# Entry of layer two in a fused two-layer network: values, keys and masks of the first two units ahead of the gathered rows

## The chip, the cores and the metric

The kernel runs on one core of a Trainium2 chip. The metric is the device time of one execution in microseconds (us), the median over a few runs. The core has a matrix engine (TensorE, PE in the profile; its weight loads are PEld), a vector engine (VectorE, DVE), an activation engine (ScalarE, ACT), a general engine (GpSimd, POOL) and a queue engine (SyncE, SP), which here only issues DMA transfers. Each engine works through its own list of instructions in order, and they wait for one another by semaphores.

## The reference, cut to what matters

Two layers act on `x`, 128 sequences of 64 tokens of 128 numbers. Each layer is attention over a context followed by a mixture of experts. In the first layer the mixture sends each token to one of 8 experts; in the second it is a soft mixture of 16 projections with an attention of its own.

```python
x = x + tanh(g_xattn[0]) * L0_xattn(layernorm(x), ctx, ctx, ...)
x = x + tanh(g_ffn[0])   * L0_ffn(layernorm(x), ...)      # one of 8 experts for each token
x = x + tanh(g_xattn[1]) * L1_xattn(layernorm(x), ctx, ctx, mask, ...)
x = x + tanh(g_ffn[1])   * L1_ffn(layernorm(x), ...)      # 16 projections, weighed
```

`L1_xattn` is attention with 16 heads of width 8. Queries come from the normed `x`, keys and values from `ctx`, which does not depend on `x`. A causal mask and a padding mask are set on the scores before the softmax:

```python
q = query @ Wq.T + bq;  k = key @ Wk.T + bk;  v = value @ Wv.T + bv
scores = einsum('bhtd,bhsd->bhts', q, k) * 8 ** -0.5
scores = where(causal_mask | key_padding_mask, neg_inf, scores)
out = einsum('bhts,bhsd->bhtd', softmax(scores), v) @ Wo.T + bo
```

## The kernel before, in words

The 8192 tokens are 32 units of 256 tokens (4 sequences). Layer one's attention loops over the units. Its mixture scatters the token rows to DRAM sorted by expert, and a loop over 71 slots of 128 rows (`slots`) reads them in that order, computes, and stores them in `sorted_out`. Layer two takes the rows of a unit back with two indirect transfers (`gather`), which POOL issues once the last slots are stored. `upper_units` then runs layer two's steady loop (`body1`), in which the mixture of unit u is interleaved with the attention of the units u+1 to u+5. Each engine has such a body, written by hand.

Between the slots and `body1` stands the entry of layer two, an order written out by hand for every engine. It brings units 0 and 1 through attention and starts units 2 and 3. This entry alone is what the change touches. Its steps by name:

- `gather(v)` (POOL): the rows of unit v into `xin`. `first_stats` (DVE), `norm` (POOL) and `apply_norm` (ACT) make the normed rows `xn`.
- `upper_in(v)` (PE) transposes them into the PSUM bank `m0`, `copy_xT` (ACT) copies them to `xcT`. `upper_queries_keys(v)` (PE) multiplies by `wq` and `wk` into the left and the right half of the bank `m1`; `queries` and `keys` (ACT) copy these to `qT` and `kT`, and `place_keys` (SP) moves `kT` to `kx` with four transfers. There is one `kT` and one `kx`. The keys of unit 0 are made during the slots already, through the semaphore `first_keys`.
- `upper_values(v)` (PE, `head_values`) makes the values in `m0` from the context in `xcT`, and `copy_v` (ACT) copies them to `vb`.
- `pad_row(v)` (POOL) makes the mask of unit v in `mask_keys`. `upper_scores` (PE) adds it to the four score banks `s_bank` with eight matmuls, and `head_products` adds the products of `qT` and `kx` to it with 16.
- `max_bank` (DVE), `subtract_bank` (PE), `exp_bank` (ACT), `upper_probs` (PE, transposes into the one bank `tb`), `copy_pT` (ACT) and `upper_weigh` (PE) are softmax and weighing, for four quads of heads j = 0 to 3.

A float32 matmul stands twice in the trace for each call, so that 16 calls of `head_products` are rows with x32.

Of the kernel before, what the change touches and what calls it, by code (L numbers as in the profile page):

```python
# [32 lines left out]
SLOTS = N // P + E0 - 1  # L33
# [44 lines left out]
def flamingo(nc, a, out):  # L78
    ctx = ExitStack()
    with ctx:  # L80
# [44 lines left out]
        wk = [sb(f"wk{l}", [P, P]) for l in range(2)]  # L125
# [31 lines left out]
        xcT = [sb(f"xcT{b}", [P, 2, UNIT]) for b in range(2)]  # L157
# [41 lines left out]
        moved = sb("moved", [P, E0 - 1])  # L199
# [55 lines left out]
        m1 = bank("m1")  # L255
# [54 lines left out]
        def wait(eng, semaphore, count):  # L310

            if not isinstance(count, int) or count > 0:
                eng.wait_ge(semaphore, count)
# [78 lines left out]
        def _(sp):  # L392
# [7 lines left out]
            def place_keys(layer, v):  # L400

                q = s[layer]
                sp.wait_ge(q["k_ready"], v + 1)
                for r in range(4):
                    sp.dma_start(kx[r:P:4, r, :], kT[r:P:4, :]).then_inc(q["keys_placed"], 16)

# [111 lines left out]
        def _(g):  # L518
# [159 lines left out]
            slots(g, slot, split=lower_proj, late=1)  # L678
            g.wait_ge(setup["similarity_steps"], 3)
            g.tensor_tensor(simn[:, :], simq[:, :], half_pos[:, :], ALU.pow).then_inc(setup["similarity_steps"], 1)  # L680
            g.wait_ge(routed["moved"], 1)
            for k in range(3):
                g.wait_ge(stored[k], 16 * ((SLOTS + 2 - k) // 3))

            def hidden_norm(v):

# [42 lines left out]
            def body1(u):  # L729
# [15 lines left out]
                hidden_length(u + 2)  # L745
                add(u, "o", 2, 3)

            gather(0)
            gather(1)
            norm(1, 0)  # L750
            pad_row(0)
            residual(1, 0, 0)
            norm(1, 1)
            pad_row(1)
            gather(2)
            residual(1, 1, 1)
            norm(1, 2)
# [14 lines left out]
        def _(act):  # L772
# [26 lines left out]
            def keys(layer, v):  # L799
                q = s[layer]  # L800
                if exists(v):
                    if layer == 1 and v == 0:
                        act.wait_ge(f["first_keys"], 1)
                    else:
                        act.wait_ge(q["qk_in_psum"], v + 1)
                    wait(act, q["keys_placed"], 64 * v)
                    wait(act, q["scores_in_psum"], 4 * v)
                    act.activation(kT[:, :], m1[:, 256:512], ACT.Identity,
                                   bias=bcol[:, 2 * layer + 1:2 * layer + 2]).then_inc(q["k_ready"], 1)

# [230 lines left out]
                apply_second_norm(1, u + 2, lambda t: x3[(u + 2) % 5][:, t, :], lambda t: hn[:, t, :])  # L1041

            q = s[1]
            apply_norm(1, 0, 0)
            copy_xT(0)
            queries(1, 0)
            copy_v(q, 0, 0)
            apply_norm(1, 1, 1)
            copy_xT(1)
            exp_bank(0, 0)  # L1050
            keys(1, 1)
            exp_bank(0, 1)
            queries(1, 1)
            copy_pT(q, 0, 0)
            exp_bank(0, 2)
            copy_pT(q, 0, 1)
            exp_bank(0, 3)
            copy_v(q, 1, 1)
            copy_pT(q, 0, 2)
            copy_pT(q, 0, 3)  # L1060
            apply_norm(1, 2, 0)
# [489 lines left out]
        def _(pe):  # L1551
# [404 lines left out]
            def upper_queries_keys(v):  # L1956

                if exists(v):
                    since((v - 4, f["qk1_ready"], v - 3), (v - 2, s[1]["x_mid_ready"], v - 1), (v - 1, s[1]["k_ready"], v),
                          (v, s[1]["k_ready"], v + 1))  # L1960
                    pe.wait_ge(s[1]["xcT_ready"], v + 1)
                    pe.wait_ge(ctx_loaded[1][v % 2], 8 * (v - v % 2 + 2))
                    ins = pe.matmul(m1[:, 0:256], wq[1][:, :], xcT[v % 2][:, 0, :], start=True, stop=True)
                    if v > 0:
                        ins = pe.matmul(m1[:, 256:512], wk[1][:, :], xcT[v % 2][:, 1, :], start=True, stop=True)
                    ins.then_inc(s[1]["qk_in_psum"], 1)

# [6 lines left out]
                        ins = pe.matmul(m1[:, P * t:P * t + P], oT[:, t, :], wo[1][:, :], start=True, stop=True)  # L1974
                    ins.then_inc(s[1]["y_in_psum"], 1)

            def upper_scores(u):

                v = u + 2
                if exists(v):  # L1980
                    pe.wait_ge(s[1]["pad_row_ready"], v + 1)
                    wait(pe, s[1]["exp_ready"], 4 * v)
                    for t in range(2):
                        wait(pe, dense_used[t], parts_until(u))
                    for t in range(2):
                        mask = mask_keys[v % 2][:, 2 * t:2 * t + 2, :].rearrange("p h q -> p (h q)")
                        for j in (0, 2, 1, 3):
                            keys = slice(LEN * (j // 2), LEN * (j // 2) + LEN)
                            pe.matmul(s_bank[j][:, UNIT * t:UNIT * t + UNIT], mask[keys, :],  # L1989
                                      bcast(identb[keys, keys], 4, 1), start=(t == 0), stop=False,  # L1990
                                      skip_group_check=True)
                    head_products(s[1], v)

            def subtract_bank(v, j):

# [20 lines left out]
            def body1(u):  # L2016
# [60 lines left out]
                outputs_parts(u, 1, 3)  # L2077
                upper_in(u + 4)

            upper_in(0)  # L2080
            upper_queries_keys(0)
            upper_values(0)
            upper_scores(-2)
            upper_in(1)
            for j in SUBTRACTED[0:2]:
                subtract_bank(0, j)
# [2 lines left out]
            for j in SUBTRACTED[2:4]:  # L2089
                subtract_bank(0, j)  # L2090
            upper_probs(0, 0)
            upper_values(1)
            upper_probs(0, 1)
            upper_weigh(0, 0)
            upper_probs(0, 2)
            upper_weigh(0, 1)
            upper_probs(0, 3)
            upper_weigh(0, 2)
            upper_weigh(0, 3)
            upper_scores(-1)  # L2100
            upper_heads(0)
            subtract_bank(1, SUBTRACTED[0])
            pe.wait_ge(s[1]["qk_ready"], 2)
# [43 lines left out]
```

## Time and profile before

| | |
|---|---|
| median of 3 runs | 1690.09 us (1688.3 to 1690.72) |
| the profiled execution, its own time | 1690.68 us |
| its span, first to last instruction | 1689.0 us |
| PE, DVE, ACT, POOL busy | 94%, 72%, 64%, 70% of the span |
| mean granted clock of TensorE | 0.976 of full speed |
| last matmul of the slots ends, steady loop's first part begins | about 544.6 us, about 588.5 us |

Times in the rows are in us from the start of the span unless marked ns. The granted clock is 1.00 at 2.4 GHz and 0.50 at 1.2 GHz. In a row of the timeline the brackets at the end say how long the engine had been idle before it, and who released it. The entry takes 44 us of 1689.

### The profile page before, as it was taken

Reading aid. Unit: us, or ns where it says so; the run is one execution under the profiler, and the core shown is the slowest. Engines: PE = TensorE matmul, PEld = TensorE weight load, DVE = VectorE, ACT = ScalarE, POOL = GpSimd, SP = SyncE. Lnnn points to the kernel's source line nnn. Section 1 sums busy time; section 2 is a strip of 40 time slices with the busy share of each in tenths; the row PEclk is TensorE's granted clock in tenths of the full one; section 3 lists DMA queues with packets and bytes.
Section 4 is the critical chain, followed back from the end, with each engine's and each line's share of the span. In section 5 each row is a group of like instructions: output and inputs, shape, how many; then the busy total and the mean of one; then the engine's idle time right before and its main releaser. Section 6 shows DMA issues by size and latency. Waiting matters only on the chain.

```text
span 1689.0 us, 50848 instructions
## 1 busy us (share of the span) xinstructions
PE 1590.5 (94%) x15944; PEld 1388.4 (82%) x15945; DVE 1208.1 (72%) x3915; ACT 1079.9 (64%) x2725; POOL 1179.0 (70%) x1715
## 2 busy tenths in 40 slices
PE   6999999986998689999999999999999999999996
PEld 4777777765998479888888898889888889888885
DVE  3677777753555357887888888888788888877785
ACT  3777777753555456666666666666666666766654
POOL 3555555532455567888888888888788878887785
PEclk9999999986999899999999999999999999999998
DMA  2322222234553100000000000000000000000000
GB/s 74 108 70 71 70 69 75 75 108 113 145 140 84 30 14 17 14 17 17 20 15 17 17 18 17 17 17 14 20 14 17 17 20 14 17 17 11 5 8 10
DMA packets 92101, 68.95 MB, mean 41 GB/s; under 512 B 13936, under 2 KB 87696, under 8 KB 91920
## 3 DMA queue, kind: packets, MB, share of 16 engines
q1 hardware_dynamic: 76512, 49.34, 10.0%
q0 software_dynamic: 5120, 12.62, 2.4%
q10 hardware_dynamic: 10288, 4.74, 1.0%
q8 instruction: 94, 1.54, 0.4%
q14 instruction: 87, 0.71, 0.1%
HBM read 35.74 MB, written 22.52 MB: 34 GB/s over the span
## 4 chain that ended last, share of the span: by engine, by line
PE 84%; DVE 6%; issue 4%; POOL 2%; ACT 1%; DMA 1%; SPq 1%; DVEq 0%; POOLq 0%; ACTq 0%
PE s_bank L1858 13%; PE s_bank L1859 12%; PE s_bank L1860 12%; PE po L1682 8%; PE tb L1667 6%; PE s_bank L1800 4%; PE po L1812 4%; PE s_bank L1647 4%; PE s_bank L1998 2%; PE m L1621 1%; PE m L1708 1%; PE s_bank L1989 1%; PE tb L1858 1%; PE m L1606 1%; PE s_bank L1656 1%
## 5 line engine op out<-in xcount | busy, mean ns | idle before, releaser
L727 POOL TENSOR_TENSOR qkv<-qkv,scaled 128x384 f32<-128x384 f32 x480 | 490.3, 1021 | 134.1 <-ACT scaled L1001 97.6
L1001 ACT ACTIVATE scaled<-s_bank,wg 128x384 f32<-128x384 f32 x448 | 256.6, 582 | 128.6 <-PE s_bank L1860 127.1
L1858 PE MATMUL s_bank<-proj_hi,hn_hi 128*128 128x384 f32 x896 | 329.8, 368 | 1.2 <-DVE qkv L1440 0.9
L1440 DVE SCALAR_TENSOR_TENSOR qkv<-s_bank,wg,qkv 128x384 f32<-128x384 f32 x448 | 273.6, 611 | 49.0 <-PE s_bank L1860 37.6
L1859 PE MATMUL s_bank<-proj_lo,hn_hi 128*128 128x384 f32 x896 | 302.4, 337 | 0.0
L1860 PE MATMUL s_bank<-proj_hi,hn_lo 128*128 128x384 f32 x896 | 300.9, 336 | 0.0
L862 ACT ACTIVATE pT<-tb 128x512 f32<-128x512 f32 x256 | 152.1, 594 | 164.7 <-PE tb L1667 97.2
L1858 PEld LDWEIGHTS s_bank<-proj_hi,hn_hi 128*128 128x128 f32 x896 | 168.6, 188 | 15.8 <-ACT scaled L1001 5.9
L1859 PEld LDWEIGHTS s_bank<-proj_lo,hn_hi 128*128 128x128 f32 x896 | 169.3, 189 | 3.0
L1860 PEld LDWEIGHTS s_bank<-proj_hi,hn_lo 128*128 128x128 f32 x896 | 168.3, 188 | 0.0
L1667 PE MATMUL tb<-ident,prob 128*128 128x128 f32 x1024 | 157.6, 277 | 5.2 <-ACT pT L862 5.0
L1682 PEld LDWEIGHTS po<-vb,pT 128*64 128x64 f32 x4096 | 139.0, 138 | 22.4 <-issue 22.4
L1682 PE MATMUL po<-vb,pT 128*64 128x18 f32 x4096 | 152.0, 213 | 0.5 <-ACT pT L862 0.5
L1451 DVE SCALAR_TENSOR_TENSOR halves<-s_bank,wg,halves 128x128 f32<-128x128 f32 x448 | 127.4, 343 | 24.5 <-DVE halves L1451 19.7
L1667 PEld LDWEIGHTS tb<-ident,prob 128*128 128x128 f32 x1024 | 118.2, 141 | 29.2 <-issue 19.9
L727 POOL TENSOR_TENSOR sums<-sums,scaled 128x512 f32<-128x512 f32 x96 | 123.3, 1285 | 11.9 <-ACT scaled L1005 6.0
L1005 ACT ACTIVATE scaled<-s_bank,wg 128x128 f32<-128x128 f32 x384 | 109.6, 369 | 24.3 <-PE s_bank L1860 23.9
L948 ACT ACTIVATE prob<-s_bank 128x512 f32<-128x512 f32 x128 | 73.5, 600 | 80.1 <-PE s_bank L1998 80.1
L919 ACT ACTIVATE hT<-s_bank,b_cols 128x128 f32<-128x128 f32 x284 | 81.1, 368 | 62.5 <-PE s_bank L1800 62.4
L650 POOL DMA_INDIRECT sorted_in<-xr,posi x64 | 66.1, 1033 | 67.3 <-DVE posi L1236 53.6
L1394 DVE TENSOR_REDUCE mx<-s_bank 128x8 fp32r<-128x512 f32 x128 | 79.4, 682 | 45.5 <-PE s_bank L1647 45.5
L1171 DVE RECIPROCAL rden<-po 128x32 f32<-128x32 f32 x64 | 22.8, 357 | 120.8 <-PE po L1682 120.8
(284 smaller groups left out, 3819.8 us busy)
## 6 DMA issues: line engine op xcount, KB each, us to landing
xs<-sorted_in SPq DMA_DIRECT2D x71, 128.5 KB, 2.1
kx<-kT SPq DMA_DIRECT2D x256, 32.0 KB
sorted_out<-yo SPq DMA_DIRECT2D x71, 64.0 KB, 1.6
xin<-in_x SPq DMA_DIRECT2D x32, 128.0 KB
cin<-in_ctx SPq DMA_DIRECT2D x32, 128.0 KB, 2.3
ctx_cols<-xcT SPq DMA_DIRECT2D x32, 128.0 KB
w<-in_L_ffn_W SPq DMA_DIRECT2D x16, 256.0 KB, 3.9
xcT<-ctx_cols SPq DMA_DIRECT2D x32, 128.0 KB, 2.3
```

Source lines behind the costliest of these rows:

```text
L727: g.tensor_tensor(into, into, scaled[m % SCALED][:, 0:cols], ALU.add).then_inc(dense_added, 1)
L862: act.activation(pT[j % 2][:, :, :, :], tb[:, :].rearrange("p (r t n) -> p r t n", r=2, t=2), ACT.Copy).then_inc(q["probT_ready"], 1)
L919: ins = act.activation(hT[1 - par][:, cols], s_bank[1 - par][:, cols], ACT.Gelu, bias=b1_cols[:, bass.ds(e * FJ + j, 1)])
L1001: ins = act.activation(into, bank[:, 0:3 * D], ACT.Copy, scale=wg[v % 4][:, 1, k:k + 1])
L1005: ins = act.activation(part[:, cols] if k else sums[:, e, :], bank[:, cols], ACT.Copy, scale=wg[v % 4][:, 1, 4 * k + e:4 * k + e + 1])
L1440: v.scalar_tensor_tensor(out=acc, in0=bank[:, 0:3 * D], scalar=wg[w % 4][:, 0, k:k + 1], in1=acc, op0=ALU.mult, op1=ALU.add).then_inc(dens ...
L1451: ins = v.scalar_tensor_tensor(out=into, in0=bank[:, cols], scalar=wg[w % 4][:, 0, e:e + 1], in1=into, op0=ALU.mult, op1=ALU.add)
L1667: ins = pe.transpose(tb[:, col:col + P], prob[j][:, t, 2 * r:2 * r + 2, :], ident[:, :])
L1682: ins = pe.matmul(po[64 * half:64 * half + 64, col:col + 2 * VW], pT[j % 2][:, t, r, 64 * half:64 * half + 64], vb[par][:, seq, 2 * j + r, ...
L1858: pe.matmul(bank[:, 0:cols], hi[:, tile], of(proj_hi), start=True, stop=False)
L1859: pe.matmul(bank[:, 0:cols], hi[:, tile], of(proj_lo), start=False, stop=False)
L1860: pe.matmul(bank[:, 0:cols], lo[:, tile], of(proj_hi), start=False, stop=True)\
```

## The change

Everything in the entry that needs only the context is put ahead of what needs the gathered rows. PE makes the values of unit 0, the keys of unit 1 (`second_keys`), the values of unit 1 and the masks of unit 0 before `upper_in(0)`. ACT copies these three results before its first `apply_norm`. POOL makes both masks before it waits for the stored slots. Unit 1's keys then lie in `kT` while unit 0's are still in `kx`, so SP waits for unit 0's scores before it moves them. The masks of unit 1 go onto the score banks before `upper_weigh(0, 2)`, and the products of unit 1 follow unit 0's weighings as before.

```diff
@@ place_keys (SP)
                 sp.wait_ge(q["k_ready"], v + 1)
+                if layer == 1 and v == 1:
+                    sp.wait_ge(q["scores_in_psum"], 4)
@@ entry, POOL
-            g.wait_ge(routed["moved"], 1)
-            for k in range(3):
-                g.wait_ge(stored[k], 16 * ((SLOTS + 2 - k) // 3))
...
+            pad_row(0)
+            g.wait_ge(s[1]["pad_row_ready"], 1)
+            pad_row(1)
+            g.wait_ge(routed["moved"], 1)
+            for k in range(3):
+                g.wait_ge(stored[k], 16 * ((SLOTS + 2 - k) // 3))
             gather(0)
             gather(1)
             norm(1, 0)
-            pad_row(0)
             residual(1, 0, 0)
             norm(1, 1)
-            pad_row(1)
             gather(2)
@@ keys (ACT)
-                    if layer == 1 and v == 0:
-                        act.wait_ge(f["first_keys"], 1)
+                    if layer == 1 and v < 2:
+                        act.wait_ge(f["first_keys"], v + 1)
+                        wait(act, q["keys_placed"], 64 * v)
                     else:
                         act.wait_ge(q["qk_in_psum"], v + 1)
-                    wait(act, q["keys_placed"], 64 * v)
-                    wait(act, q["scores_in_psum"], 4 * v)
+                        wait(act, q["keys_placed"], 64 * v)
+                        wait(act, q["scores_in_psum"], 4 * v)
@@ upper_queries_keys (PE)
-                    if v > 0:
+                    if v > 1:
                         ins = pe.matmul(m1[:, 256:512], wk[1][:, :], xcT[v % 2][:, 1, :], start=True, stop=True)
@@ new (PE)
+            def second_keys():
+
+                pe.wait_ge(s[1]["k_ready"], 1)
+                pe.wait_ge(ctx_loaded[1][1], 16)
+                pe.matmul(m1[:, 256:512], wk[1][:, :], xcT[1][:, 1, :], start=True, stop=True).then_inc(f["first_keys"], 1)
```

`upper_scores` is split in the change into `upper_masks(u)` and `head_products`; the steady loop still calls both together. What the hand-written orders become is shown by the instructions themselves.

PE at the start of the entry, before: the first row is the transpose of unit 0's normed rows. L1953 is `upper_in`, L1963 and L1965 the queries and keys, L1621 the values, L1989 the masks, L1647 the products, L1998 the subtraction of the maxima.

```order
L1953 MATMUL m<-ident,xn 128x128 [waits xn_ready_1,moe_y_ready]
L1953 MATMUL m<-ident,xn 128x128
L1963 MATMUL m<-xcT,wq 128x256 [waits ctx_loaded_1_0,xcT_ready_1,k_ready_1]
L1621 MATMUL m<-wv,xcT 64x64 [waits ctx_loaded_1_0]
L1621 MATMUL m<-wv,xcT 64x64 x7
L1989 MATMUL s_bank<-identb,mask_keys 128x256 [waits pad_row_ready_1]
L1989 MATMUL s_bank<-identb,mask_keys 128x256 x7
L1647 MATMUL s_bank<-kx,qT 64x256 [waits keys_placed_1,qk_ready_1]
L1647 MATMUL s_bank<-kx,qT 64x256 x15
```

The same place in the change, with the lines of the new file (L1625 the values, L1985 `second_keys`, L1999 the masks, L1957 `upper_in`, L1967 the queries, L1651 the products):

```order
L1625 MATMUL m<-wv,xcT 64x64 [waits ctx_loaded_1_0,moe_y_ready]
L1625 MATMUL m<-wv,xcT 64x64 x7
L1985 MATMUL m<-xcT,wk 128x256 [waits ctx_loaded_1_1,k_ready_1]
L1625 MATMUL m<-wv,xcT 64x64 [waits ctx_loaded_1_1,v_ready_1]
L1625 MATMUL m<-wv,xcT 64x64 x7
L1999 MATMUL s_bank<-identb,mask_keys 128x256 [waits pad_row_ready_1]
L1999 MATMUL s_bank<-identb,mask_keys 128x256 x7
L1957 MATMUL m<-ident,xn 128x128 [waits xn_ready_1,v_ready_1]
L1957 MATMUL m<-ident,xn 128x128
L1967 MATMUL m<-xcT,wq 128x256 [waits ctx_loaded_1_0,xcT_ready_1,k_ready_1]
L1651 MATMUL s_bank<-kx,qT 64x256 [waits keys_placed_1,qk_ready_1]
L1651 MATMUL s_bank<-kx,qT 64x256 x15
```

Values and masks no longer stand between the query matmul and the products of unit 0.

ACT while it works on unit 0's softmax, before (L948 is `exp_bank`, L808 `keys`, L816 `queries`, L862 `copy_pT`, L825 `copy_v`):

```order
L948 ACTIVATE prob<-s_bank 128x512 [waits scores_ready_1]
L808 ACTIVATE kT<-m,bcol 128x256 [waits scores_in_psum_1,keys_placed_1,qk_in_psum_1]
L948 ACTIVATE prob<-s_bank 128x512 [waits scores_ready_1]
L816 ACTIVATE qT<-m,bcol 128x256 [waits scores_in_psum_1,qk_in_psum_1]
L862 ACTIVATE pT<-tb 128x512 [waits probT_in_psum_1]
L948 ACTIVATE prob<-s_bank 128x512 [waits scores_ready_1]
L862 ACTIVATE pT<-tb 128x512 [waits probT_in_psum_1]
L948 ACTIVATE prob<-s_bank 128x512 [waits scores_ready_1]
L825 ACTIVATE vb<-m 64x32x8 [waits v_in_psum_1]
L825 ACTIVATE vb<-m 64x32x8
L862 ACTIVATE pT<-tb 128x512 [waits pv_in_psum_1,probT_in_psum_1] x2
```

And the same in the change (L952 `exp_bank`, L820 `queries`, L866 `copy_pT`):

```order
L952 ACTIVATE prob<-s_bank 128x512 [waits scores_ready_1] x2
L820 ACTIVATE qT<-m,bcol 128x256 [waits scores_in_psum_1,qk_in_psum_1]
L866 ACTIVATE pT<-tb 128x512 [waits probT_in_psum_1]
L952 ACTIVATE prob<-s_bank 128x512 [waits scores_ready_1]
L866 ACTIVATE pT<-tb 128x512 [waits probT_in_psum_1]
L952 ACTIVATE prob<-s_bank 128x512 [waits scores_ready_1]
L866 ACTIVATE pT<-tb 128x512 [waits pv_in_psum_1,probT_in_psum_1] x2
```

Unit 1's key copy and value copy are gone from between the exponentials and the copies of the transposed probabilities.

## Rows read from the trace of the kernel before

**Rows 1.** The page: busy time, and the chain that ended last, by engine.

```profile
PE 1590.5 (94%) x15944; PEld 1388.4 (82%) x15945; DVE 1208.1 (72%) x3915; ACT 1079.9 (64%) x2725; POOL 1179.0 (70%) x1715
...
PE 84%; DVE 6%; issue 4%; POOL 2%; ACT 1%; DMA 1%; SPq 1%; DVEq 0%; POOLq 0%; ACTq 0%
```

**Rows 2.** The chain in order of time, entry: start us, us, what.

```profile
555.83 0.66 PE m L1953 x2
...
557.01 1.19 PE m L1963 x2
558.21 1.05 PE m L1621 x16
559.26 0.97 PE s_bank L1989 x8
560.23 1.42 PE s_bank L1647 x32
...
572.16 1.21 PE s_bank L1647 x32
```

**Rows 3.** Timeline of the entry, DVE, ACT and PE: start, us, instruction.

```profile
558.24 0.47 ACT L816 ACTIVATE qT<-m,bcol 128x256 f32<-128x256 f32 x1 [1.33 <-PE m L1963]
...
561.67 2.48 DVE L1394 TENSOR_REDUCE mx<-s_bank 128x8 fp32r<-128x512 f32 x4 [4.96 <-PE s_bank L1647]
...
565.60 0.60 ACT L862 ACTIVATE pT<-tb 128x512 f32<-128x512 f32 x1
...
567.99 0.80 ACT L825 ACTIVATE vb<-m 64x256 f32<-64x256 f32 x2
...
568.82 0.60 ACT L862 ACTIVATE pT<-tb 128x512 f32<-128x512 f32 x1
...
570.12 0.67 PE L1682 MATMUL po<-vb,pT 128*64 128x18 f32 x16
570.23 0.60 ACT L862 ACTIVATE pT<-tb 128x512 f32<-128x512 f32 x1 [0.81 <-PE tb L1667]
```

**Rows 4.** Timeline of the entry, POOL and SP's queue.

```profile
536.98 2.94 POOL L680 TENSOR_TENSOR simn<-simq,half_pos 128x16 f32<-128x16 f32 x1
...
548.06 1.15 POOL L579 DMA_INDIRECT xin<-sorted_out,placei  x1 [8.14 <-issue]
...
554.85 0.61 POOL L593 TENSOR_TENSOR pad_unit<-not_causal,pad_keys 128x256 f32<-128x256 f32 x1
555.54 0.72 POOL L596 TENSOR_TENSOR mask_keys<-pad_unit,causal 128x256 bf16<-128x256 f32 x1
...
564.90 2.84 SPq L405 DMA_DIRECT2D kx<-kT  x4
```

**Rows 5.** Stretches: length, busy PE, PEld, DVE, ACT, POOL, granted clock, DMA, GB/s.

```profile
30.00:35.00 5.00, 4.57 (x55) 3.27 (x56) 2.48 (x4) 1.19 (x2) 2.78 (x10) 0.50 0.47 159
370.00:377.00 7.00, 5.70 (x47) 4.92 (x48) 1.93 (x12) 2.01 (x6) 2.02 (x2) 0.50 0.11 40
547.00:555.00 8.00, 0.00 (x0) 0.00 (x0) 0.73 (x4) 0.19 (x1) 5.64 (x9) 0.50 0.12 33
557.00:560.00 3.00, 2.99 (x26) 1.86 (x26) 0.00 (x0) 1.16 (x3) 2.54 (x6) 0.50 0.00 0
560.00:561.00 1.00, 1.00 (x28) 0.64 (x32) 0.00 (x0) 0.97 (x3) 0.91 (x1) 0.70 0.37 130
584.00:588.00 4.00, 1.30 (x18) 0.88 (x12) 2.13 (x15) 2.00 (x6) 0.63 (x1) 0.99 0.21 66
588.00:591.00 3.00, 3.00 (x14) 2.33 (x14) 2.36 (x10) 0.44 (x2) 0.44 (x2) 0.50 0.03 5
626.00:1600.00 974.00, 972.76 (x8485) 864.63 (x8470) 782.21 (x2246) 654.31 (x1646) 794.27 (x1013) 1.00 0.06 16
```

**Rows 6.** Timeline, PE at half clock in layer one.

```profile
30.43 2.02 PE L1647 MATMUL s_bank<-kx,qT 32*64 32x256 f32 x32 [3.27 <-DMA kx<-kT]
32.37 1.11 PE L1667 MATMUL tb<-ident,prob 128*128 128x128 f32 x4
```

More of the change, by code:

```diff
@@ L1043, in _ @@
             q = s[1]
+            copy_v(q, 0, 0)
+            keys(1, 1)
+            copy_v(q, 1, 1)
             apply_norm(1, 0, 0)
@@ L1046, in _ @@
             queries(1, 0)
-            copy_v(q, 0, 0)
             apply_norm(1, 1, 1)
@@ L1050, in _ @@
             exp_bank(0, 0)
-            keys(1, 1)
             exp_bank(0, 1)
@@ L1057, in _ @@
             exp_bank(0, 3)
-            copy_v(q, 1, 1)
             copy_pT(q, 0, 2)
@@ L1975, in upper_output, with upper_masks @@
                     ins.then_inc(s[1]["y_in_psum"], 1)
-            def upper_scores(u):
+            def second_keys():
+                pe.wait_ge(s[1]["k_ready"], 1)
+                pe.wait_ge(ctx_loaded[1][1], 16)
+                pe.matmul(m1[:, 256:512], wk[1][:, :], xcT[1][:, 1, :], start=True, stop=True).then_inc(f["first_keys"], 1)
+            def upper_masks(u):
                 v = u + 2
@@ L1991, in upper_scores @@
                                       skip_group_check=True)
-                    head_products(s[1], v)
+            def upper_scores(u):
+                upper_masks(u)
+                head_products(s[1], u + 2)
             def subtract_bank(v, j):
@@ L2078, in body1 @@
                 upper_in(u + 4)
+            upper_values(0)
+            second_keys()
+            pe.wait_ge(s[1]["v_ready"], 1)
+            upper_values(1)
+            upper_masks(-2)
+            pe.wait_ge(s[1]["v_ready"], 2)
             upper_in(0)
             upper_queries_keys(0)
-            upper_values(0)
-            upper_scores(-2)
+            head_products(s[1], 0)
             upper_in(1)
@@ L2091, in _ @@
             upper_probs(0, 0)
-            upper_values(1)
             upper_probs(0, 1)
@@ L2097, in _ @@
             upper_probs(0, 3)
+            upper_masks(-1)
             upper_weigh(0, 2)
             upper_weigh(0, 3)
-            upper_scores(-1)
+            head_products(s[1], 1)
             upper_heads(0)
```

## The prediction

> **What bounds the kernel now.** I read the page first. PE is busy 94% of the span, and 84% of the chain that ended last runs over it [rows 1]. Then I read the stretches. From 626 to 1600 us PE is busy 972.76 of 974 us at full clock [rows 5]. The steady loop is thus bound by PE, and the change touches no instruction of it. What the entry saves moves the whole loop forward by the same amount; it can't grow there, and nothing in a full PE takes it back. So the question is only how much earlier the steady loop starts.
>
> In the entry the chain in order of time is the view that counts. PE transposes unit 0's normed rows at 555.83, makes the queries at 557.01, and then works through values (1.05 us) and masks (0.97 us) until the products of unit 0 begin at 560.23 [rows 2]. The queries' copy `qT` begins at 558.24 and takes 0.47 us, so `qT` is there at 558.71 [rows 3]. The products need nothing else of these, so values and masks stand on the path although they need no gathered row.
>
> The stretches show a second thing. From 547 to 555 PE does nothing and its granted clock is at 0.50. It is still at 0.50 from 557 to 560, and in the microsecond from 560 it is 0.70 on average, so it rises at 560.6 [rows 5]. The first steps of the entry run at 1.2 GHz.
>
> **The change part by part.**
>
> *What is put ahead.* PE's two sets of values, the keys of unit 1 and the masks of unit 0 go to the 11 us between the last slot (544.6) and the first transpose (555.83 [rows 2]). At the rows' half-clock durations that is 1.05 twice, 1.19 for the keys (the query matmul has the same shape) and 0.97, together 4.3 us, plus three copies on ACT of 0.80, 0.47 and 0.80 [rows 2, 3]. Even fully in series it is 6.3 us, done near 551. PE and ACT have nothing to do until the rows come, so this costs nothing. If that cover were not there, all 6.3 us would count. POOL ends its last operation of the slots at 539.9 and issues the first gather at 548.06, after 8.14 us of idling. Two masks at 0.61 + 0.72 fill 2.7 us of this [rows 4]. The gather waits for the stored slots, not for POOL, so it does not move, and neither does the first transpose. Behind `norm(1, 1)` a mask of 1.3 us no longer stands before `gather(2)`; those rows are first needed by DVE behind unit 0's maxima, so I count nothing.
>
> *Unit 0's products.* I let them start 0.10 us behind `qT` (ACT's copy started 0.04 behind the query matmul, which ended at 557.01 + 1.19 = 558.20 [rows 2, 3]), so at 558.81 instead of 560.16 to 560.23. That is 1.35 us. But they now run before the clock rises. Before, most of them ran at full clock, and from their start to the first maximum at 561.67 it was 1.44 us [rows 2, 3]. A set of products at half clock took 2.02 us [rows 6]. So they end at 560.83, and with 0.2 for the way to DVE the maxima begin at 561.04 instead of 561.67. **Term 1: -0.6 us.** At full clock the same term would be about -1.5, at most.
>
> *Keys of unit 1.* Their matmul (0.59 us at full clock, half of the 1.19 above) leaves PE between the subtractions of the maxima, and their copy (0.47 as `qT`) leaves ACT between the exponentials. Before, ACT ran exponential, key copy, exponential, query copy, and then the first copy of transposed probabilities at 565.60 [rows 3]. One copy less on ACT is 0.47. **Term 2: -0.45 us.** Bounds: zero, if the maxima on DVE (2.48 us for four [rows 3]) end last there, and -0.6, if the matmul does.
>
> *Value copy of unit 1.* It stands at 567.99 for 0.80 us ahead of the third of four copies of transposed probabilities. The third comes at 568.82, the fourth at 570.23, a distance of 1.41 [rows 3]. From the first to the fourth it is 4.63, where three distances of 1.41 are 4.23. **Term 3: -0.4 us.** PE also loses 0.7 us of values here, but it waits for ACT in this part and this adds nothing.
>
> *Masks of unit 1.* They took the place behind the weighings and now stand before the third. Before, the third weighing (570.12, 0.67 us) lay beside ACT's fourth copy (570.23, 0.60) and the fourth weighing and the masks lay behind it [rows 3]. Now the masks lie beside the copy and two weighings lie behind it. PE has the same work behind the copy to within 0.1 us. **Term 4: 0.** Bounds -0.1 and +0.1. The normalisation on DVE starts some 0.5 us later against the copy, still ahead of the maxima of unit 1.
>
> *SP's new wait.* Unit 1's keys lie ready near 548, but `kx` is held by unit 0's until its products end. SP then issues four transfers in 2.84 us [rows 4], from about 561 to 564, some 4 us earlier than at 564.90 before. Behind them on SP stands a context load of unit 3, needed much later. The products of unit 1 at about 571 find their keys. Cost 0.
>
> The sum is -0.6 - 0.45 - 0.4 = -1.45 us, for a clock that rises at the same place as before.
>
> **What the clock does to the sum.** This I can't take over. At 560.6 the clock rose behind work without a gap: 2.99 us busy of the 3 from 557 to 560. In the change PE is without work from 558.2 (end of the query matmul) to 558.8, waiting for `qT`. From 370 to 377 PE was busy 5.70 of 7 us, with such gaps, and the clock stayed at 0.50; from 30 to 35 it rose only at the end of a stretch that had become continuous [rows 5]. So I take the rise to come a few microseconds later, near 564, which is an estimate. The query matmul of unit 1 then takes 1.19 instead of 0.59 and the subtractions are slower, part of which hides behind the maxima. I take +0.35 for it. **The forecast is -1.1 us.** Against the profiled execution's own time, 1690.68, this gives 1689.6; that execution lies 0.6 above the median of 1690.09, so against the median it is 1689.0.
>
> What the Trainium skill says on this speaks against the change. In "TensorE: Matmul & The Clock Gate", section "HAM oscillation — how this bites in real kernels", work in short bursts between waits pays the return from the half clock again and again. By it the early work buys no warm clock, since idling follows it, and what is left behind the rows is thinner and warms the engine later. The idle stretch from 547 to 555 at 0.50 agrees with it; the time that it gives is that of the first rival below.
>
> **The rivals.**
>
> *The clock stays low through unit 0's softmax (25%).* For it: by moving about 2.6 us of values, masks and keys away, PE's work between 557 and 568 gets more gaps, and rows 5 show a stretch of 7 us with gaps that did not raise it. Against: from 564 on PE has transposes and weighings for ACT to feed on, and at half clock these fill it. Price: from -1.45, +0.6 for the matmul of the queries, +0.4 for subtractions, and for each of one to four quads a transposing of 1.11 instead of 0.60 [rows 6], so +0.5 to +2.0. This gives +0.05 to +1.55 us, 1690.1 to 1691.6: slower than before from the second quad on, by less than can be measured. It decides from the point at which the low clock reaches past 566 us.
>
> *A later low stretch goes too (12%).* After PE idled in 584 to 588 (busy 1.30 of 4), it ran 588 to 591 at half clock, busy throughout [rows 5]. If the earlier entry moves this idle time so that the clock does not fall, up to 1.6 us come on top; a second such place stands at the first unit of the steady loop, where PE waits for POOL's sums. With -1.45 this gives -3.0 to -4.5, 1685.6 to 1687.1. For it: the clock fell only at the end of that idle stretch. Against: the stretch keeps its length.
>
> *The work was hidden anyway or does not arrive (8%).* If the maxima, which keep their 2.48 us, and the softmax of unit 1 set the end alone, only term 1 counts and is eaten by the clock: -0.3 to 0, 1689.8 to 1690.1. The rows of ACT's copies, 1.41 apart with ACT and PE in turn, speak against it.
>
> The remaining 55% are the forecast, with an own range of -1.5 to -0.6, 1688.6 to 1689.5.
>
> **How the numbers follow.** A measurement of this kernel tells about 0.2%, 3.4 us, from no change. Every case but the upper part of the second rival lies within that; faster by more would be below 1686.7, and only that rival with both low stretches reaches it. The three runs of before lie 2.4 us apart, which I add as scatter on both sides. Faster 9%, same 87%, slower 4% (the low clock through all quads together with scatter). The range reaches from the middle of the second rival, 1686.8, to the upper part of the first, 1691.4.
>
> **What the changed profile would show.** Values, keys and masks between 545 and 551 us; the first gather at 548 and the first transpose near 555.8 as before; unit 0's products about 0.1 us behind `qT` and 2 us long; the first copy of `pT` at 564.5 to 565.2, the four copies 1.41 apart; unit 1's products without a wait for keys at about 571; the first part of the steady loop at 587.0 to 587.9 instead of 588.5. Wrong it would be if the first transpose came later than 556 (a wait among the early work), if unit 1's products waited for `kx`, or if the clock's rise lay beyond 567.

## The result and the profile after

The changed kernel takes 1695.5 us (median of 6 runs, 1693.25 to 1697.62), the kernel before 1689.66 us (6 runs, 1685.53 to 1690.93). The ratio is 1.003, with a 95% interval of 1.002 to 1.004: slower by 0.3%, where 1689.0 us was forecast and 1691.4 was the end of the range. The profiled execution has a span of 1694.5 us, with a mean granted clock of 0.971 (0.976 before).

The chain that ended last is the first view again. This is the changed kernel's, in the entry (start us, us, what); it answers to [rows 2].

```profile
557.33 0.48 ACT qT L820
557.81 0.04 issue
557.86 2.17 PE s_bank L1651 x32
...
563.90 0.87 PE tb L1671 x4
...
565.53 1.09 PE tb L1671 x4
566.62 1.00 PE po L1686 x16
...
570.71 0.96 PE s_bank L1999 x6
571.68 1.85 PE po L1686 x32
573.52 2.10 PE s_bank L1651 x32
```

The first lines are as forecast. The products of unit 0 start right behind `qT`, 2.94 us behind the first transpose (557.86 - 554.92), where it was 4.33 (560.16 - 555.83). But then the PE steps in the chain take 1.5 to 1.7 times as long: the transposes of a quad 1.09 us where they took 0.65, a weighing 1.00 where it took 0.65. Before, the chain alternated between ACT and PE at this point:

```profile
566.35 0.65 PE tb L1667 x4
567.02 0.60 ACT pT L862
...
570.97 0.65 PE po L1682 x16
```

In the change it lies on PE alone from 565.53 on, up to unit 1's maxima at 575.65. Before, unit 1's products began 16.27 us behind the first transpose; here it is 18.54.

The stretches say why. These are of the changed kernel, with the columns of [rows 5] (the clock is the third number from the end).

```profile
545.00:549.00 4.00, 2.12 (x36) 1.28 (x32) 0.54 (x3) 2.07 (x5) 1.54 (x2) 1.00 0.06 16
549.00:555.00 6.00, 0.08 (x1) 0.11 (x2) 0.82 (x5) 0.88 (x2) 4.72 (x8) 0.55 0.16 44
555.00:560.00 5.00, 3.92 (x37) 1.76 (x38) 0.65 (x4) 1.62 (x4) 2.67 (x6) 0.50 0.09 26
560.00:566.00 6.00, 4.91 (x15) 3.28 (x15) 3.21 (x8) 2.92 (x6) 2.83 (x7) 0.50 0.22 66
566.00:573.00 7.00, 7.00 (x77) 5.38 (x78) 0.00 (x0) 3.04 (x6) 2.05 (x2) 0.50 0.08 22
573.00:580.00 7.00, 6.69 (x57) 4.59 (x56) 4.50 (x12) 1.75 (x4) 0.23 (x2) 0.50 0.00 0
580.00:581.00 1.00, 0.52 (x3) 0.20 (x1) 0.67 (x4) 0.44 (x1) 0.87 (x2) 0.84 0.02 8
...
592.00:597.00 5.00, 5.00 (x44) 3.72 (x51) 2.37 (x10) 0.97 (x3) 1.29 (x4) 0.50 0.01 3
```

The column to read is the clock. It falls at 549.6 and rises at 580.3, so that it is low for 30.7 us, where before it was 13.7 us (to 560.6, [rows 5]). All of unit 0's softmax and the first half of unit 1's run at 1.2 GHz. Two low stretches follow around the start of the steady loop, from 590.6 and from 624.7. Each is 6.8 us long, where before there were two of 3.4 us, from 587.9 and from 622.0.

A measure free of what happens in layer one is the distance from the first transpose to the first part of the steady loop: 588.52 - 555.83 = 32.69 us before, 592.85 - 554.92 = 37.93 after, 5.2 us more. The spans differ by 5.5 us: 0.9 less up to the first transpose, 5.2 more in the entry, and 1.2 more from there to the end (1101.7 us against 1100.5). From the end of the last slot to the first transpose it is 11.22 us in both, so the early work did not delay the rows.

### The profile page after: what moved, and what is told of

Its sections match the earlier page's. It is cut to its first block, busy times and chain, and to the rows that moved or that the text cites. A ratio compares the mean times of both kernels' runs of the same rounds, so it can differ in the third digit from the quotient of the medians.

```text
span 1694.5 us, 50853 instructions
## 1 busy us (share of the span) xinstructions
PE 1601.3 (94%) x15944; PEld 1394.6 (82%) x15945; DVE 1209.7 (71%) x3915; ACT 1082.3 (64%) x2725; POOL 1179.1 (70%) x1715
## 4 chain that ended last, share of the span: by engine, by line
PE 86%; DVE 5%; issue 3%; POOL 2%; ACT 1%; DMA 1%; SPq 0%; DVEq 0%; POOLq 0%; ACTq 0%
PE s_bank L1862 14%; PE s_bank L1863 12%; PE s_bank L1864 12%; PE po L1686 8%; PE tb L1671 6%; PE s_bank L1651 4%; PE s_bank L1804 4%; PE po L1816 4%; PE s_bank L2012 2%; PE m L1625 1%; PE m L1712 1%; PE m L1610 1%; PE s_bank L1999 1%; PE tb L1862 1%; PE s_bank L1660 1%
## 5 line engine op out<-in xcount | busy, mean ns | idle before, releaser
L866 ACT ACTIVATE pT<-tb 128x512 f32<-128x512 f32 x256 | 152.3, 595 | 166.2 <-PE tb L1671 98.6
L952 ACT ACTIVATE prob<-s_bank 128x512 f32<-128x512 f32 x128 | 73.4, 600 | 81.7 <-PE s_bank L2012 81.7
```

The source lines that it names most:

```text
L866: act.activation(pT[j % 2][:, :, :, :], tb[:, :].rearrange("p (r t n) -> p r t n", r=2, t=2), ACT.Copy).then_inc(q["probT_ready"], 1)
```

## The experiments

Two theories stood against each other. The clock theory: what was moved away is PE work of the microseconds in which the engine's clock had risen before, and the low clock costs the time. The order theory: the new order itself makes waits (masks ahead of two weighings, products without cover), and the clock only follows. All extra matmuls below are one function, put into PE's entry; nobody reads what they write.

```python
def fill(n):
    for _ in range(n):
        pe.matmul(tb[:, :], onesb[:, :], bcast(identb[:, :], 4, 1), start=True, stop=True)
```

Results of all runs are in one table; "unit 1" is the distance in us from the first transpose to unit 1's products, "loop" that to the steady loop's first part, both from the one profiled execution. Rows under one line were timed together on one chip, and the line gives the median of the kernel before, timed beside them (for the first two rows no chip is on record). The last two groups carry the same chip number on record, though the kernel before took 1799.62 us in one and 1689.21 us in the other.

A single execution also scatters by what lies ahead of the entry: among the profiles at the usual times the first transpose stands between 551.4 and 557.0 us. The distances are free of this, the medians are not.

| kernel | median us | ratio to before, 95% | unit 1 | loop |
|---|---|---|---|---|
| before, first profile | 1689.66 | 1 | 16.27 | 32.69 |
| the change, first profile | 1695.5 | 1.003 (1.002 to 1.004) | 18.54 | 37.93 |
| --- | | before 1689.87 | | |
| e1_warm_after | 1686.47 | 0.9981 (0.9972 to 0.999) | 12.68 | 29.31 |
| e2_warm_before | 1687.43 | 0.9987 (0.9979 to 0.9996) | 14.44 | 30.72 |
| e3_dense_gap | 1688.69 | 0.9993 (0.9984 to 1.0002) | 15.09 | 31.97 |
| e4_masks_back | 1692.08 | 1.002 (1.0007 to 1.0032) | 18.53 | 37.93 |
| --- | | before 1692.05 | | |
| e5_change_again | 1693.38 | 1.0007 (0.9992 to 1.0021) | 18.54 | 36.05 |
| e6_masks0_back | 1689.22 | 0.9988 (0.9979 to 0.9997) | 15.75 | 32.60 |
| e7_fill_early | 1689.93 | 0.9992 (0.9979 to 1.0004) | 15.60 | 32.22 |
| e8_warm_masks_back | 1686.88 | 0.9972 (0.9962 to 0.9981) | 13.05 | 29.67 |
| --- | | before 1799.62 | | |
| e9_light_fill | 1795.05 | 0.9973 (0.9959 to 0.9987) | 17.12 | 33.99 |
| e10_warm_all_after | 1788.62 | 0.9938 (0.9915 to 0.9961) | 12.69 | 29.81 |
| e11_warm_all_before | 1789.59 | 0.9941 (0.9921 to 0.9961) | 14.44 | 30.83 |
| e12_pool_alone | 1795.08 | 0.9977 (0.9962 to 0.9992) | 17.16 | 33.79 |
| --- | | before 1689.21 | | |
| e13_change_third | 1690.34 | 1.001 (0.9997 to 1.0023) | 15.04 | 31.91 |
| e14_fill_early_again | 1689.82 | 1.0012 (0.9999 to 1.0026) | 15.03 | 31.91 |
| e15_pool_alone_again | 1688.94 | 1.0001 (0.9992 to 1.001) | 16.14 | 32.57 |
| e16_warm_all_again | 1682.15 | 0.9962 (0.9946 to 0.9977) | 12.67 | 28.95 |

**e1_warm_after.** 

> The changed kernel with 32 extra matmuls (128x512 bf16, into the bank tb, whose contents nobody reads before they are overwritten) on PE between unit 0's early masks and the first transpose, about 7 us that PE idled. Clock theory (the half clock from 549.6 to 580.3 us costs the time): the granted clock stays at 1.00 into the entry, unit 1's products begin about 14.5 us behind the first transpose instead of 18.5, and the whole takes 1685 to 1689 us. Order theory (the new order itself makes waits, the clock only follows): the same distance of 18 us or more and 1694 us or more.

```diff
             upper_masks(-2)
+            fill(32)
             pe.wait_ge(s[1]["v_ready"], 2)
             upper_in(0)
```

The extra work makes the kernel 0.19% faster than the kernel before, within the 1685 to 1689 us of the clock theory. The stretches of this kernel:

```profile
545.00:556.00 11.00, 9.84 (x77) 4.86 (x76) 2.31 (x11) 2.93 (x9) 5.93 (x9) 1.00 0.13 36
556.00:560.00 4.00, 2.23 (x37) 1.10 (x36) 0.73 (x4) 2.15 (x6) 1.66 (x6) 1.00 0.12 36
560.00:570.00 10.00, 8.31 (x128) 6.04 (x128) 3.82 (x10) 5.96 (x12) 6.20 (x9) 1.00 0.18 49
570.00:584.00 14.00, 10.16 (x136) 7.80 (x120) 7.65 (x35) 8.12 (x19) 6.37 (x15) 1.00 0.04 13
584.00:588.00 4.00, 3.43 (x15) 3.14 (x16) 1.88 (x10) 1.53 (x4) 0.00 (x0) 0.57 0.15 43
```

The clock stays at 1.00 up to 584. Its timeline, PE and ACT in unit 0's softmax, with the first transpose at 556.56:

```profile
558.73 1.12 PE L1651 MATMUL s_bank<-kx,qT 32*64 32x256 f32 x32 [0.56 <-ACT qT L820]
...
566.23 0.67 PE L1686 MATMUL po<-vb,pT 128*64 128x18 f32 x16
566.34 0.60 ACT L866 ACTIVATE pT<-tb 128x512 f32<-128x512 f32 x1 [0.32 <-PE tb L1671]
567.08 0.63 PE L1671 MATMUL tb<-ident,prob 128*128 128x128 f32 x4 [0.18 <-ACT pT L866]
567.64 0.61 PE L1999 MATMUL s_bank<-identb,mask_keys 64*128 64x256 bf16 x8
567.74 0.60 ACT L866 ACTIVATE pT<-tb 128x512 f32<-128x512 f32 x1 [0.81 <-PE tb L1671]
568.18 1.13 PE L1686 MATMUL po<-vb,pT 128*64 128x18 f32 x32
569.24 1.12 PE L1651 MATMUL s_bank<-kx,qT 32*64 32x256 f32 x32
```

From the first transpose on these are the same instructions in the same order as in the change. The products take 1.12 instead of 2.01, the copies are 1.40 apart instead of up to 2.05, and unit 1's products come at 12.68 us instead of 18.54, better than the 14.5 that was expected. A theory that blames the order can't explain this.

**e2_warm_before.** 

> The kernel before with 44 of the same extra matmuls ahead of the first transpose (9.4 us). Clock theory: the low stretch of 13.7 us goes, the first steps of the entry run at full clock, unit 1's products begin 14 to 15 us behind the first transpose instead of 16.3, and the whole takes 1687 to 1688.5 us; the changed order with a warm clock stays 1 to 2 us below it. Order theory: no change from before, 1689 to 1690 us, and clearly below the changed order.

```diff
+            fill(44)
             upper_in(0)
             upper_queries_keys(0)
             upper_values(0)
```

As expected: 1687.43 us and 14.44 us to unit 1's products. Lines of its timeline:

```profile
551.44 0.44 PE L1953 MATMUL m<-ident,xn 128*128 128x128 f32 x2 [0.63 <-ACT xn L844]
...
554.15 1.12 PE L1647 MATMUL s_bank<-kx,qT 32*64 32x256 f32 x32
...
555.46 2.48 DVE L1394 TENSOR_REDUCE mx<-s_bank 128x8 fp32r<-128x512 f32 x4 [3.06 <-PE s_bank L1647]
...
564.01 0.60 ACT L862 ACTIVATE pT<-tb 128x512 f32<-128x512 f32 x1 [0.81 <-PE tb L1667]
...
565.88 1.12 PE L1647 MATMUL s_bank<-kx,qT 32*64 32x256 f32 x32
```

With the clock held high in both, the changed order is 14.44 - 12.68 = 1.76 us ahead there and 1.41 us ahead at the loop. So in the entry the change saves about what it was forecast to save (1.45 us), when the clock does not differ. The medians lie 1 us apart the same way, but their intervals overlap.

**e3_dense_gap.** 

> The changed kernel with 5 of the extra matmuls between the query matmul of unit 0 and its products, 2.1 us at half clock, of which 0.6 lie in the wait for qT and 1.5 on the path. Clock theory: PE's work is dense again where values and masks stood, the clock rises before 566 us, and the run is faster than the change although work was added to its path: 1690 to 1693 us. Order theory: 1.5 us slower than the change, 1697 us.

```diff
             upper_queries_keys(0)
+            fill(5)
             head_products(s[1], 0)
```

The extra matmuls in its timeline, and then stretches of this kernel:

```profile
556.69 2.34 PE L2097 MATMUL tb<-identb,onesb 128*128 128x512 bf16 x5
```

```profile
550.00:554.00 4.00, 0.00 (x0) 0.00 (x0) 0.73 (x4) 0.50 (x2) 3.35 (x7) 0.50 0.16 43
555.00:559.00 4.00, 3.48 (x15) 1.30 (x14) 0.25 (x3) 1.62 (x4) 2.37 (x5) 0.50 0.10 33
559.00:560.00 1.00, 1.00 (x33) 0.60 (x32) 0.00 (x0) 0.00 (x0) 0.69 (x2) 0.87 0.24 57
560.00:573.00 13.00, 10.54 (x147) 7.44 (x139) 5.99 (x14) 6.50 (x14) 4.48 (x8) 1.00 0.14 39
```

There is useless work on the path, 1.5 us of it (products at 4.44 instead of 2.94), and yet all 11 runs lie between 1685.0 and 1689.9, below the 1690 to 1693 us that were expected. The clock rises at 559.3, and unit 1's products come at 15.09. The change without this work has 18.54 there in one kind of execution and, as e13 will show, 15.04 in another. So the five matmuls don't make an execution faster than the change's good ones. What they do is that no slow one is left: no run of 11 has a mean clock below 0.975. The order theory had put it at 1697 us.

**e4_masks_back.** 

> The changed kernel with unit 1's masks back behind unit 0's weighings, as before. Clock theory: no change beyond scatter, 1694.5 to 1696.5 us, the clock low until about 580. Order theory (two weighings behind the masks delay the products of unit 1): 1.5 us or more faster, below 1694 us.

```diff
-            upper_masks(-1)
             upper_weigh(0, 2)
             upper_weigh(0, 3)
+            upper_masks(-1)
```

The profile agrees with the change to 0.01 us (18.53, 37.93), as the clock theory says. The median does not: 1692.08, where the order theory had put it (below 1694 us). But its 12 runs fall into two groups, seven from 1689.0 to 1692.4 and five from 1696.5 to 1697.4, and the profiled run of the upper group has the distances of the change. By the median alone this run decides nothing, so the change had to be run again beside the next ones.

**e5_change_again.** 

> The changed kernel itself once more, on the chip of the next three, as their base. Clock theory and order theory alike: 1693 to 1698 us.

No edit. Twelve runs from 1688.28 to 1699.58. Five are at or below 1690.01 with a mean clock of 0.976 or 0.977, and seven from 1692.35 up with 0.969 to 0.972. The change has no one time. In its profile, of a run of 1696.72 us, the clock was low from 554.2 to 578.1.

**e6_masks0_back.** 

> The changed kernel with one part undone: PE adds unit 0's masks again between the query matmul and the products (POOL still makes them early). 1.0 us of PE work at half clock comes back, 0.45 of it onto the path. Clock theory: PE has no gap there any more, the clock rises near 560 to 566 as before, and the run is faster than the change: 1688 to 1691 us. Order theory: 0.5 us slower than the change.

```diff
             upper_values(1)
-            upper_masks(-2)
             pe.wait_ge(s[1]["v_ready"], 2)
             upper_in(0)
             upper_queries_keys(0)
+            upper_masks(-2)
             head_products(s[1], 0)
```

One part undone, products 0.33 us later (3.27), and the median is 4.2 us below the change's on the same chip. Its slowest run is at 1693.77, and no run has a mean clock of 0.972 or less, where seven of twelve of the change had. As expected.

**e7_fill_early** and **e14_fill_early_again.** 

> As e1_warm_after, but with 8 of the extra matmuls instead of 32, so that they end near 549 us and PE idles about 5.5 us before the first transpose. Clock theory (what counts is PE's work right before the rows come, not the extra instructions): the clock is at 0.50 again when the rows come, and the time is that of the change, 1693 to 1698 us. If the extra instructions themselves help: 1687 us.

```diff
-            fill(32)
+            fill(8)
```

> e7_fill_early again. If its 1689.9 was chance: a median within 1.5 us of the change's on the same chip. If early dense work helps by itself: 3 us or more below the change, and few executions above 1693 us.

The expectation for e7 was missed: 1689.93, with one of 11 runs above 1694. Beside the change on one chip, e14 had 1689.82 against 1690.34 for e13: three of its twelve runs are above 1694, and the profiles of the two agree to 0.01 us (15.03 and 15.04; 31.91 both). So e7 had probably drawn mostly good executions. Of both together 5 of 23 runs have a mean clock of 0.972 or less, of the change beside them 11 of 24; a small help is neither shown nor excluded.

**e8_warm_masks_back.** 

> e1_warm_after with unit 1's masks back behind unit 0's weighings. At full clock term 4 of the prediction says no difference: within 0.5 us of 1686.5. Order theory (the masks in their new place cost time): 1 us or more below.

The edit of e4 on top of e1. The times agree within scatter; in the profile the masks' old place is 0.37 us worse (13.05 against 12.68). So the new place is no cost, but a small gain.

**e9_light_fill.** 

> e1_warm_after with the same 32 extra matmuls made light: 8 columns instead of 512. Clock theory: they are over within 2 us and PE idles before the rows, so the clock is at 0.50 then and the time spreads like the change's own, some executions near 1688 and some at 1694 or more, mean clock of the slow ones 0.972 or less. If extra instructions as such help: all within 1685 to 1688 as e1_warm_after.

```diff
-                    pe.matmul(tb[:, :], onesb[:, :], bcast(identb[:, :], 4, 1), start=True, stop=True)
+                    pe.matmul(tb[:, 0:8], onesb[:, :], identb[:, 0:8], start=True, stop=True)
```

In this group of runs the kernel before took 1799.62 us, so only distances and ratios compare, and the ratios with care (see e12). The clock was at 0.50 when the rows came, and the distances are 17.12 and 33.99, where the full fill of e10 on the same chip had 12.69 and 29.81. So 32 extra instructions as such don't help. The two groups of times that were expected were not to be seen (all 12 runs from 1791.1 to 1796.9).

**e10_warm_all_after** and **e16_warm_all_again.** 

> e1_warm_after with 9 more extra matmuls in the wait before unit 1's heads (2.1 us) and 14 in the first unit of the steady loop, where PE waits 3.4 us for POOL's sums. Clock theory: the low stretches near 585 and 620 us go too, each had about 3.4 to 6.8 us at half clock with PE full; 2 to 4 us below e1_warm_after, 1683 to 1685 us. If these stretches are hidden: no change from 1686.5.

```diff
             def body1(u):
+                if u == 1:
+                    fill(14)
                 token_transposes(u - 1)
...
             upper_values(2)
+            fill(9)
             upper_heads(1)
```

> The changed order with all three fills, again. Clock theory: the low stretches at the entry, near 585 and near 620 us are gone, 1683 to 1685 us, 5 us or more below the kernel before.

In the last group e16 takes 1682.15 us, somewhat less than the 1683 to 1685 that were expected. That is 0.38% below the kernel before (interval 0.23% to 0.54%) and 8.2 us below the change in the same group. Stretches of e16:

```profile
541.00:552.00 11.00, 9.57 (x75) 4.74 (x74) 2.32 (x11) 2.97 (x8) 6.27 (x9) 1.00 0.13 34
552.00:582.00 30.00, 24.40 (x304) 17.24 (x305) 13.14 (x52) 17.44 (x40) 13.93 (x28) 1.00 0.12 33
582.00:586.00 4.00, 2.99 (x48) 1.74 (x46) 3.18 (x9) 1.21 (x3) 1.62 (x5) 1.00 0.00 0
586.00:616.00 30.00, 28.21 (x228) 24.66 (x227) 16.60 (x53) 15.97 (x35) 23.16 (x32) 1.00 0.05 14
616.00:626.00 10.00, 10.00 (x92) 8.52 (x90) 6.63 (x15) 6.52 (x15) 5.33 (x8) 1.00 0.06 17
```

Not one low stretch is left between 541 and 1600. This version beats both kernels.

**e11_warm_all_before.** 

> The order of before with all three fills (44, 9 and 14 extra matmuls). Clock theory: 1684.5 to 1686.5 us, 1 to 2 us above the changed order with the same fills, since terms 1 to 3 of the prediction (at full clock 1.5 + 0.45 + 0.4 us) then stand alone. Order theory: at or below the changed order.

The order of before with `fill` at the same three places: 1 us above e10 in the median, inside the scatter of both, and 1.0 us behind it at the loop (30.83 against 29.81), 1.75 at unit 1's products. So most of the gain is the clock's, not the order's. The ratios of this group, 0.9938 and 0.9941, may be too good, though: e16, which is e10 again, has 0.9962.

**e12_pool_alone** and **e15_pool_alone_again.** 

> The kernel before with POOL's part of the change alone: both masks made ahead of the wait for the stored slots. No theory sees a cost in it: PE's work and its clock are as before, 1689 to 1690.5 us. If it is 1 us or more off, POOL's part has an effect that I did not count.

```diff
+            pad_row(0)
+            g.wait_ge(s[1]["pad_row_ready"], 1)
+            pad_row(1)
+            g.wait_ge(routed["moved"], 1)
+            for k in range(3):
+                g.wait_ge(stored[k], 16 * ((SLOTS + 2 - k) // 3))
             gather(0)
             gather(1)
             norm(1, 0)
-            pad_row(0)
             residual(1, 0, 0)
             norm(1, 1)
-            pad_row(1)
```

> POOL's part of the change alone, again. No effect: within 1 us of the kernel before on the same chip. An effect of its own: 3 us or more below it, as on the slower chip.

The 0.23% of e12, outside its expectation, did not come again: e15 has 1688.94 against 1689.21, ratio 1.0001, and distances of 16.14 and 32.57 like those of before. POOL's part is neutral. What differed in the slow group stays open; in e12's profile PE was busy for 908.97 of 940 us in the steady loop (760 to 1700), in e15's for 899.52 of 900 (700 to 1600), so that this loop was not as full there.

**e13_change_third.** 

> The changed kernel a third time, as the base of the next. Executions in two groups: some at 1688 to 1690 us with a mean clock of 0.976 or more, most at 1693 to 1700 us with 0.972 or less; median 1693 to 1696 us.

1690.34 us, lower than expected; four of 12 runs have a mean clock of 0.972 or less, and the other eight lie from 1687.6 to 1693.6. One of the four is the profiled run, with 1690.82 us and 0.972. In the entry it is nevertheless of the good kind, with an early rise: it lost its clock elsewhere, with about 51 us of low clock ahead of the entry, where the profile of before has 44. The mean clock is a sign of the late rise, not a proof. Stretches and timeline:

```profile
552.00:556.00 4.00, 0.00 (x0) 0.00 (x0) 0.73 (x4) 0.88 (x2) 3.21 (x7) 0.50 0.12 33
556.00:560.00 4.00, 2.81 (x27) 1.44 (x34) 0.73 (x4) 1.62 (x4) 1.78 (x5) 0.50 0.09 24
560.00:564.00 4.00, 3.69 (x31) 1.98 (x15) 2.75 (x6) 0.96 (x3) 2.36 (x3) 0.50 0.23 66
564.00:565.00 1.00, 1.00 (x5) 0.77 (x4) 0.45 (x4) 0.87 (x3) 0.25 (x2) 0.65 0.10 33
565.00:573.00 8.00, 6.50 (x122) 4.68 (x120) 1.33 (x3) 4.46 (x9) 3.15 (x5) 1.00 0.13 36
```

```profile
559.05 2.01 PE L1651 MATMUL s_bank<-kx,qT 32*64 32x256 f32 x32 [0.56 <-ACT qT L820]
...
561.25 2.48 DVE L1398 TENSOR_REDUCE mx<-s_bank 128x8 fp32r<-128x512 f32 x4 [4.26 <-PE s_bank L1651]
...
565.43 0.60 ACT L866 ACTIVATE pT<-tb 128x512 f32<-128x512 f32 x1 [0.56 <-PE tb L1671]
...
569.65 0.60 ACT L866 ACTIVATE pT<-tb 128x512 f32<-128x512 f32 x1 [0.81 <-PE tb L1671]
570.09 1.13 PE L1686 MATMUL po<-vb,pT 128*64 128x18 f32 x32
571.15 1.12 PE L1651 MATMUL s_bank<-kx,qT 32*64 32x256 f32 x32
```

The first transpose is at 556.11, and the clock rises at 564.7. Here the change is 16.27 - 15.04 = 1.23 us ahead of [rows 2] at unit 1's products and 0.78 at the loop. It does not arrive at the end: the span is 1689.1 us, that of before 1689.0. The first transpose came 0.3 us later, and 0.6 was lost behind the start of the loop. The two low stretches there, from 585.2 and from 619.3, are 6.8 us long here too.

## Why the prediction was wrong

- **What bounds the kernel: right in the main.** The steady loop passed the entry's loss on; from 632 to 1606 us PE was busy 973.51 of 974 us. But "nothing in a full PE takes it back" left out the loop's start. From there to the end it took 1100.5 us before, 1101.7 in the change and 1101.1 in e13. Over the other profiles at the usual times it is 1100.0 to 1102.3 (1098.6 in e16, without low stretches), so that a gain of 1 us drowns there; what sets it is not shown.
- **What is put ahead costs nothing: right in itself.** Values, keys and masks ended at 547.4 in the changed profile, earlier than the 551 of the forecast, since the clock was still at 1.00. The gather and the first transpose kept their distance to the last slot (11.22 us), and e15 shows no effect of POOL's part. Wrong was that this price list held only durations. The work also had a use where it stood. With the masks back in their place (e6) or five useless matmuls in it (e3) no run of 22 had a mean clock of 0.972 or less.
- **Term 1, unit 0's products: right with a low clock.** Forecast -0.6 at the maxima, measured in e13 (561.25 - 556.11) - (561.67 - 555.83) = -0.70, and a set of products of 2.01 us. Its bound was wrong: at full clock it was said to be about -1.5, and e1 against e2 shows 2.71 - 2.17 = 0.54 at the products' start, since the values and masks that leave the path are then short too.
- **Terms 2 and 3: right.** With the clock held high (e1 against e2) the way from the maxima to the first copy of `pT` is 3.49 us instead of 3.93, which is -0.44 for term 2, and from the first copy to the fourth 4.22 instead of 4.62, -0.40 for term 3. In e13 these four copies take 4.22 too, where it was 4.63.
- **Term 4: too small.** Forecast 0 with bounds of 0.1. From the fourth copy to unit 1's products it is 1.50 us in e1 and in e13, 1.87 in e2 and before: -0.37, which e8 confirms.
- **SP's wait: right.** Unit 1's products waited for no keys in any profile.
- **What the clock does to the sum: this step failed.** It took the rise "a few microseconds later, near 564" and added 0.35 us. In the first measurement the clock rose at 580.3 instead. Against before, this made +0.81 us from the maxima to the first copy of `pT`, +1.33 over the four copies, +0.84 from there to unit 1's products and +2.97 from these to the loop. With term 1's -0.71 this is +5.24, in place of -1.1. In e5's profile the clock rose 21.0 us behind the first transpose (25.4 in the first), and it was +3.4 us at the loop. This is no rare accident: 16 of the change's 30 timed runs have a mean clock of 0.972 or less (the profiled one of e13 wrongly among them), against none of the 98 runs of the kernel before that were timed beside the experiments at the usual times (0.974 and more).
- **Where the rise was met, the sum came out by luck.** In e13 the clock rose at 564.7, and unit 1's products were 1.23 us ahead, near the forecast's 1.1. But from the maxima to the first copy it is 4.18 us, where it was 3.93. With term 2's -0.44 taken off, the low clock had cost 0.69 and not 0.35 there, and term 4's uncounted 0.37 made up for it.
- **The first rival had the mechanism and not its size.** It let the low clock end with unit 0's softmax, at most 1.55 us above before, and gave it 25%. Even at unit 1's products it was 2.27 us (18.54 - 16.27): the rival priced slower transposes, but not the weighings and unit 1's masks (1.00 and 0.96 us in the chain above), which stood on the path too. It argued that transposes and weighings would fill PE and so end the low clock. They did fill it, 7.00 of 7 us from 566 to 573, and the clock stayed at 0.50. So it reached into unit 1's softmax as well, where nothing had been priced.
- **The Trainium skill** had been weighed and ranked behind the forecast. Its page "TensorE: Matmul & The Clock Gate", section "HAM oscillation — how this bites in real kernels", says that work in bursts between waits pays the return from the half clock again and again. The profiles agree in part: the change's entry is such a burst, and filling the wait ahead of it (e1) or one gap in it (e3) removed the loss. That the clock stayed at 0.50 while PE was busy for 7.00 of 7 us does not follow from it.

Left open: what decides between the two kinds of execution of one and the same kernel. Up to unit 0's softmax they are nearly alike. The clock fell 5.3 us ahead of the first transpose in the first profile and 5.1 us ahead in e13, and the maxima began 5.13 and 5.14 us behind it; then it rose at 25.4 us in one and at 8.6 us in the other. The runs show the shares, not the cause.

## What to carry to other kernels

Before work is moved off an engine's path, ask what clock the engine has there and what raised it. In a latency-bound entry behind an idle stretch, TensorE work that looks superfluous on the path may be what brings the clock back; price the step at both clocks, to the end of the stretch, and not only to the next change of phase. Where TensorE must wait for rows anyway, extra matmuls into a free bank cost nothing here and gained 0.2%, at three such places 0.4%. Don't take a gain at the start of a full loop for a gain at its end: in e13 0.78 us did not arrive. And time a kernel whose clock rises by chance often enough to see both groups: three measurements of the change gave ratios of 1.003, 1.0007 and 1.001, the first with five of its six runs at a mean clock of 0.972 or less.

## What the runs showed of the hardware that was not expected

PE was at work almost without a gap and its clock stayed low: in the changed kernel it was busy 7.00 of 7 us and then 6.69 of 7 with transposes, weighings, masks and products, at 0.50. In e3 it rose 2.6 us behind the start of five matmuls of 512 columns; in e13, without them, 3.9 us later in relation to the first transpose. The same kernel differs by 11.3 us between executions on one chip (e5, 1688.28 to 1699.58), and there the mean granted clock tells the groups apart (0.976 and more, 0.972 and less). And one group of runs took some 6% longer with every kernel, the kernel before 1799.62 us, yet with the same distances in a warm entry (12.69 and 14.44 us to unit 1's products, 12.68 and 14.44 elsewhere). Without the extra matmuls the distance was longer there too: 17.16 us in e12 against 16.14 in e15, the same kernel.
